# Layer 0 of a four-layer cross-attention kernel: its probabilities are turned by DMA in two-byte planes in place of TensorE

## The reference

```python
q = rmsnorm(x, gq) @ wq.T            # 16 heads of 64
k, v = rmsnorm(ctx, gkv) @ wk.T, ... # 4 heads of 64, each used by 4 query heads
p = softmax(q k^T / 8)               # 112 x 375 for each head and batch
x = x + (p v) @ wo.T
```

## Time and profile before

| | |
|---|---|
| time, median of 3 runs | 4849.15 us (4848.43 to 4851.47) |
| the profiled execution's own time | 4847.86 us |
| its span, first to last instruction | 4846.1 us |
| mean granted TensorE clock | 0.955 of full speed |
| busy share of the span: PE, ACT, DVE, POOL | 92%, 61%, 61%, 47% |
| one stream of layer 0 (16 pairs) | 57.70 us |

### The profile page before, as it was taken

How to read it: one execution, slowest core, us unless ns; L and a number is a source line. 1 busy time by engine, 2 the same in 40 slices (tenths; PEclk the granted TensorE clock), 3 DMA queues, 4 the chain that set the end, 5 groups by cost and what they waited for, 6 DMA issues and landing times.

```text
span 4846.1 us, 84907 instructions
## 1 busy us (share of the span) xinstructions
PE 4440.9 (92%) x30496; PEld 3230.0 (67%) x30496; DVE 2955.7 (61%) x6426; ACT 2974.7 (61%) x9009; POOL 2282.1 (47%) x4132
## 2 busy tenths in 40 slices
PE   8999999967787878789999999999999999999998
PEld 5666666646565656566666666666667777778777
DVE  6566566566666666666555555555555666667665
ACT  4555555688888888885444454444445666666664
POOL 3333333465656565664444444444444444444443
PEclk9999999979888888889999999999999999999999
DMA  2000000032333232343433333333332100000000
GB/s 85 21 21 24 21 21 22 25 90 62 62 61 64 61 62 63 61 86 68 98 76 77 75 74 77 77 74 74 77 76 47 41 19 19 18 19 19 18 18 7
DMA packets 631891, 249.53 MB, mean 51 GB/s; under 512 B 596784, under 2 KB 613424, under 8 KB 630064
## 3 DMA queue, kind: packets, MB, share of 16 engines
q1 hardware_dynamic: 631472, 244.10, 23.0%
HBM read 82.53 MB, written 14.68 MB: 20 GB/s over the span
## 4 chain that ended last, share of the span: by engine, by line
PE 82%; ACT 8%; POOL 4%; DVE 3%; issue 2%; DMA 2%; SPq 0%; ACTq 0%; POOLq 0%; DVEq 0%
PE ring L1437 51%; PE score L1366 11%; PE ring L1380 7%; ACT e L1563 5%; PE ring L1418 3%; PE ring L1411 3%; PE ring L1426 2%; DMA probs<-halves 2%; POOL e L1961 1%; POOL e L1964 1%; PE ring L1377 1%; PE ring L1401 1%; ACT work L1624 1%; PE ring L1452 1%; DVE nmax L1698 1%
## 5 line engine op out<-in xcount | busy, mean ns | idle before, releaser
L1964 POOL TENSOR_SCALAR e<-e,rsum 112x375 f32<-112x375 f32 (+1 forms) x2048 | 1102.2, 556 | 1677.4 <-DVE rsum L1705 1642.5
L1698 DVE TENSOR_REDUCE nmax<-score 112x2 f32<-112x750 f32 (+1 forms) x1152 | 1066.4, 951 | 407.0 <-PE score L1366 406.4
L1563 ACT ACTIVATE e<-score,nmax 112x375 f32<-112x375 f32 (+1 forms) x2048 | 1038.6, 537 | 117.8 <-DVE nmax L1698 115.5
L1437 PE MATMUL ring<-h,weights 128*128 128x224 f32 x3840 | 872.1, 369 | 34.5 <-ACT work L1624 24.9
L1437 PEld LDWEIGHTS ring<-h,weights 128*128 128x128 f32 x3840 | 734.3, 197 | 145.1 <-issue 52.7
L1366 PE MATMUL score<-keys,q 64*112 64x375 f32 (+2 forms) x3584 | 607.3, 493 | 235.4 <-ACT e L1563 231.4
L1603 ACT COPY probs<-ring 125x336 f32<-125x336 f32 (+1 forms) x625 | 252.5, 452 | 746.2 <-PE ring L1380 635.4
L1366 PEld LDWEIGHTS score<-keys,q 64*112 64x112 f32 (+2 forms) x3584 | 232.7, 166 | 539.0 <-ACT e L1563 289.5
L1437 PE MATMUL ring<-weights,ctx 128*128 128x512 f32 (+4 forms) x1536 | 587.1, 515 | 0.0
L1437 PE MATMUL ring<-ctx,weights 128*128 128x375 f32 x1536 | 567.2, 491 | 1.0 <-DVE heads L1799 0.8
L1563 ACT ACTIVATE e<-score,nmaxc,quant 112x375 f32<-112x375 f32 (+1 forms) x1024 | 555.1, 554 | 10.7
(11 more groups left out here) (128 smaller groups left out, 5782.1 us busy)
## 6 DMA issues: line engine op xcount, KB each, us to landing
ctx<-ctx_t SPq DMA_DIRECT2D x128, 375.0 KB, 3.1
out_t<-x SPq DMA_DIRECT2D x64, 224.0 KB, 2.0
x<-out_t SPq DMA_DIRECT2D x48, 224.0 KB, 2.6
weights<-weights SPq DMA_DIRECT2D x7, 1024.0 KB, 5.9
probs<-halves SPq DMA_TRANSPOSE x320, 2.7
planes<-halves SPq DMA_TRANSPOSE x256, 3.4
x<-x_t SPq DMA_DIRECT2D x16, 224.0 KB, 2.5
weights<-weights SPq DMA_DIRECT2D x1, 3328.0 KB, 11.5
```

The costliest lines, as they stand in the source:

```text
L1437: ins = pe.matmul(out_, a, b_, start=n == 0, stop=n == len(parts) - 1)
L1563: ins = nc.scalar.activation(e_of(u)[:, n * width:(n + 1) * width], score_bank(u)[0:S, n * width:(n + 1) * width], ACT.Exp, bias=minus, sc ...
L1698: ins = dve.tensor_reduce(to, src, AX, ALU.max, negate=True)
L1964: ins = nc.gpsimd.tensor_scalar(mine, mine, rsum[0:S, slot(u), n:n + 1], 0.0, ALU.mult, ALU.add)
```

## The change

Layer 0 takes the path of layer 2: `WORDS` becomes (0, 2), so its "turn" jobs (PE transposes and the copies behind them) are gone, and each of its pairs gets a split, a flip and a merge. In both layers all splits are on GpSimd and all merges on VectorE. Layer 1's flips and the splits share one ring of three slots of `halves`, so layer 1's "eight" of pair p waits for the flip of p-3 where it waited for p-4. The planner's costs for split, flip and merge are set anew, and layer 0's output projection is placed 1.0 pairs later. A pv of layer 0 is placed 4.5 pairs behind its last pair (it was 2.7; the line that says so does not change, it follows `WORDS`). Layer 0's context positions are cut in pieces of 128, 128 and 119 where they were three of 125.

```diff
-STEPSLOTS = 4
-WORDS = (2,)
-SPLIT_BY = ("V", "G")
+WORDS = (0, 2)
+SPLIT_BY = ("G",)
+MERGE_BY = "V"
 SPLITS = 3
 PLANES = 2
...
-        self.ones = [p for p in self.pairs if p.octet.layer == 1]
-        self.nth_of_one = {p: i for i, p in enumerate(self.ones)}
+        self.turned = [p for p in self.pairs if p.octet.layer == 1 or self.in_words(p.octet)]
+        self.nth_turned = {p: i for i, p in enumerate(self.turned)}
...
     def halves_before(self, p):
...
+        i = self.nth_turned[p]
+        return [self.turned[i - SPLITS]] if i >= SPLITS else []
...
-        self.row(e + 3.5, e + 4.6, [("o", layer, s, 0, m, "V") for m in range(KC)])
+        late = 1.0 if layer == 0 else 0
+        self.row(e + 3.5 + late, e + 4.6 + late, [("o", layer, s, 0, m, "V") for m in range(KC)])
...
-                self.add("split", p, by, 1.7, p.index + 1.4)
-                self.add("flip", p, "D", 4.2, p.index + 1.6)
-                self.add("merge", p, "VA", 1.45, p.index + 2.4)
+                self.add("split", p, by, 1.7 if by == "G" else 1.1, p.index + 1.4)
+                self.add("flip", p, "D", 3.5, p.index + 1.6)
+                self.add("merge", p, MERGE_BY, 0.9 if MERGE_BY == "V" else 1.2, p.index + 2.4)
...
         elif kind == "eight":
             yield "weigh", x
-            for p in self.steps_before(x):
+            for p in self.halves_before(x):
                 yield "flip", p
```

More of the change, by code:

```diff
@@ L933, in four_layers @@
         halves = sb("halves", [P, SPLITS, 4 * CHUNKS * P], U16)
-        steps = halves[:, :, :].rearrange("p a n -> p (a n)")[:, 0:STEPSLOTS * 8 * P].bitcast(BF16).rearrange(
-            "p (a n) -> p a n", a=STEPSLOTS)
         planes = sb("planes", [P, PLANES, 4 * CHUNKS * S], U16)
@@ L1116, in steps_of @@
             runs = 4 if is_own(p.octet) else CHUNKS
-            return steps[0:S, plan.nth_of_one[p] % STEPSLOTS, 0:2 * runs * P]
+            return halves[0:S, plan.nth_turned[p] % SPLITS, 0:2 * runs * P].bitcast(BF16)
         def halves_of(p):
-            return halves[0:S, plan.nth_halved[p] % SPLITS, :]
+            return halves[0:S, plan.nth_turned[p] % SPLITS, :]
         def planes_of(p):
@@ L1737, in vector_program @@
                     wait.wait_ge(weighed, nth["weigh", p])
-                    for before in plan.steps_before(p):
+                    for before in plan.halves_before(p):
                         flip_done(wait, before)
@@ L2000, in sync_program @@
                     wait.done([plan.pv_of[o] for o in plan.probs_before(p.octet)])
-                    sp.dma_start(flipped(p), steps_of(p), transpose=True).then_inc(turned[n % FLIPS], 16)
+                    sp.dma_start(flipped(p).bitcast(U16), steps_of(p).bitcast(U16), transpose=True).then_inc(turned[n % FLIPS], 16)
                 elif kind == "store":
```

## The result

| | before | after |
|---|---|---|
| median | 4849.31 us (4 runs) | 4952.40 us (4 runs, 4949.02 to 4959.67) |
| profiled execution | 4847.86 us, span 4846.1 | 4949.81 us, span 4948.0 |
| mean granted clock | 0.955 | 0.940 |

The ratio is 1.0214 (95% interval 1.0196 to 1.0232), or +103 us. That it is slower is clear; whether by more than 2% the interval leaves open. 4925 was forecast, in a range of 4858 to 5005.

What follows compares the result with a forecast made beforehand. GpSimd was taken to bound layer 0 at 60.4 us a stream, 62.3 with waits, against 57.7 before; 4847.9 + 74 (layer 0) + 2 (layer 1) + 0 (layer 2) = 4923.9, as a median 4925 us, range 4858 to 5005.

Steps and rivals of the forecast that it cites:

- GpSimd as the new bound of layer 0: Layer 0: GpSimd needs 50.8 us a stream undisturbed and 60.4 with stalls by merges, above PE's 46.4.
- the 0.60 of the prediction: Layer 0: each of 16 merges on VectorE takes 0.60 us from GpSimd, 9.6 us a stream.
- The whole length of a merge: Layer 0: upper bound, each merge blocks GpSimd for its whole 0.85 us, giving 64.4 us a stream.
- 62.3: Layer 0: us a stream with GpSimd's 60.4 at 97%; +4.6 for each of 16 streams, +74 us.
- Its waits: Layer 0: GpSimd as the bound loses 3% to waiting, reaching 97%, so 60.4 us become 62.3.
- The low sum: Layer 0: GpSimd needs 58.9 us a stream, with 0.53 us a merge and 0.05 us behind a split.
- the break-even case: Layer 0: low stalls, undisturbed folds, no queue loss: 58.0 us a stream, +5 us, 4853; chance 0.10.
- PE's clock: Layer 0: PE busy 70 to 80% and its clock under 1.00; at 0.85, PE's 54.6 us stay hidden.
- the rival in which it binds: Layer 0: the clock falls and PE binds again, +150 to +227 us; clock or queues over +120 us, chance 0.13.
- Layer 1: Layer 1: eight waits for the flip of p-3, 12.4 us against 12 at hand; +2 us in all.
- Layer 2: Layer 2: PE stays at 100% and 90.4 us a stream, GpSimd's added work is hidden; 0 us.
- The faster rival: Layer 0: merges fall into GpSimd's idle time, stalls under 0.43 us each; 4803 at 0.25 us; chance 0.11.

Runs made afterwards that it cites:

- sliver kernel: The changed kernel, but from the third octet on a merge of layer 0 copies only 64 of 1344 elements; 4852.0 us, 1.0003 of the kernel before.
- the plan with contended costs: The changed kernel, but the planner counts 1.4 us for a weigh and 1.95 for a split of layer 0; 4949.1 us.
- with slivers: The changed kernel, but from the third octet on layer 0's splits copy only 32 positions of each unit and its merges 64 elements; 4817.4 us.
- the kernel with two merges: The changed kernel, but each merge of layer 0 is done twice in a row on VectorE; 5130.8 us, 1.0579 of the kernel before.

## Why the prediction was right, step by step

*GpSimd as the new bound of layer 0*: right. Forecast were 60 to 65 us a stream and POOL over 90% busy; measured 61.93 and 93%. Measured for a pair: two splits and two weighs have 2 x 994 + 2 x 747 = 3.48 us, where 1.64 + 1.16 = 2.80 was the undisturbed price: 0.68 us more, against the 0.60 of the prediction. The sliver kernel, with 2.90 us, puts 0.58 of it on the merges and leaves 0.10, part of which may come from VectorE's scaling of x and context, which I had left out but for what the earlier trace rows held. In the stream one merge more costs 0.71 us and one merge less gives 0.40 back, where another bound soon takes over.

*The whole length of a merge.* The Trainium skill (SBUF — State Buffer, Who interferes with whom) says that of VectorE in a two-port mode and GpSimd the first to issue has the shared ports for its whole instruction, and the other is blocked. With a whole merge lost each time a stream would have needed 64.4 us before other losses. One merge more cost 0.71, less than its 0.84, in a queue that was nearly full. The prediction compared the rows with the rule wrongly: a merge that has started 0.19 or 0.09 us earlier has only 0.65 or 0.76 us left, and the rows showed 0.53 and 0.61. So the rule is 0.12 to 0.15 us above the rows, not 0.23 to 0.31. It names the pair of engines that the rows show; its price was an upper bound here.

*How close 62.3 came to 61.93* is in part luck. POOL was busy or in short gaps for 500 - 28.8 = 471.2 of 500 us, 58.4 us of a stream, and waited for reciprocals in the other 3.6. The prediction had 60.4 and 1.9. Its sum was 2 us too high: I had put 0.09 us of gap behind each split, and the trace has none there (433.28 + 2.10 = 435.38, and the weigh starts at 435.36), which is 1.4 us of a stream. Its waits were 1.7 us too low: 94% was reached and not 97%. The two errors cancel. The reason given for the waits, a merge ahead of the maxima in a plan that is too fast, is not confirmed: the plan with contended costs gained nothing that can be told from none. The low sum, too, is 58.6 from its own terms and not 58.9, and I cannot get the 58.0 of the break-even case from them; neither moves the forecast.

*PE's clock*: 0.94 in layer 0 with PE busy for 82%, above the 70 to 80% that I had named, and not the 0.85 and 75% of layer 1. It fell, as said, and stayed hidden; the rival in which it binds did not come. PE had 51.1 busy us in a stream and not 46.4. Whether its clock takes part when POOL is relieved (0.97 with slivers), no run separates.

*Layer 1*: the mechanism was named and its size was wrong. "I take +2 us in all" stands against 24 to 26. The sum itself had 12.4 us needed against 12 at hand, in one place of each stream, with 1 us a stream as the upper bound; the measured loss is 26.0/15 = 1.73 us a stream, beyond even that. A wait of 0.4 us on VectorE was counted as 0.4 us, once a stream. In the trace it is 31 waits of 1.4 us in 900 us (8 waits and 4.9 us in all in the kernel before). That each holds the maxima behind it and so ScalarE, the fullest engine of that layer, is how I read it; the runs show that the loss of the fourth slot costs the time, not the way in between. The prediction named a move of layer 1 by more than 10 us as a sign that it is wrong, and by that sign this part of it is.

*The end of layer 0*: left out. Some 12 us once, by the longer distance from a pair to its output as I read it.

*Layer 2*: right, 90.4 us a stream in both, PE 542.00 of 542.00 and POOL at 301 us, below the 342 that I had counted.

So +76 was forecast and +103 measured: of the difference of 27 us the shared ring has 24 and the end of layer 0 some 12, while the pace of layer 0 is 6 below the 74 counted and the layers behind give 4 back.

*The faster rival* needed a stall under 0.43 us for each merge; it was 0.58. Its prices were too high as well: with no stall it had -110 us, a stream of 50.8. With next to no merge the stream was 55.5 us, 2.2 less than before, and the three-slot ring and the end of layer 0 took that back: 4852.

## What to carry to other kernels

When work leaves the engine that is the bound, add up the engine that receives it at the new pace before anything else, and add the stalls that it causes at full load, not those seen while that engine was idle. A slot less in a ring costs more than its arithmetic when the wait stands in the queue of an engine that feeds the fullest one. Sums by engine told the stream within their ranges in the three kernels in which GpSimd was busy for 89 to 93%. When it was relieved they fell short in all five kernels that were given a range for it, by 1.5 to 5.5 us below the stream at their upper end; in two of these TensorE was busy for 91 and 92%. A full engine is not enough: its busy time had grown too, and the waits between the engines made up the rest.

## What the runs showed of the hardware that was not expected

A DVE copy of 128 x 1344 16-bit elements (0.84 us) lengthened GpSimd's instructions by 0.50 to 0.61 us and not by its whole length. With GpSimd busy for 93% the copy itself grew from 852 to 1093 ns on the mean, and the longest took 3041. Even a sliver of 64 elements, 173 ns at the shortest, took 492 ns on the mean beside a GpSimd that was busy for 86%, so a small copy does not escape the wait. With PE busy for 82% the granted clock was 0.94 on the mean of layer 0, with 75% it was 0.89 in layer 0 of the kernel with two merges and 0.85 in layer 1. These are means over stretches at full and at half clock.
